# Seven edits to the gate and hidden stages of a fused block (RG-LRU attention and ternary FFN): w_out split early, VectorE order, two high parts of g from PSUM

## The reference

```python
xn = layernorm(x)
# attention branch (RG-LRU)
y = gelu(xn @ w_y + b_y)
xb = xn @ w_x + b_x
conv = conv_b + sum(conv_w[k] * shifted(xb, 3 - k) for k in range(4))
gate_x = sigmoid(conv @ w_ig + b_ig)
gate_a = sigmoid(conv @ w_ag + b_ag)
log_a = -8.0 * gate_a * softplus(a_param)
a = exp(log_a)                         # 0 for the first token
mult = sqrt(1.0 - exp(2.0 * log_a))    # 1 for the first token
h[t] = a[t] * h[t-1] + gate_x * conv * mult
attn = (h * y) @ w_out + b_out
# FFN branch, weights replaced by {-1, 0, 1} times their mean absolute value
g = silu(xn @ w1q.T) * (xn @ w3q.T)    # 682 hidden features
ffn = g @ w2q.T
out = x + attn + ffn
```

## Time and profile before

| | |
|---|---|
| median of 3 runs | 74.77 us |
| lowest, highest | 74.32, 74.97 us |
| the profiled execution's own time | 74.64 us |
| span of the profiled execution | 72.8 us |
| TensorE busy with matmuls | 68.1 us (93% of the span), 378 instructions |
| VectorE busy | 56.8 us (78%), 93 instructions |
| ScalarE busy | 52.5 us (72%), 81 instructions |
| GpSimd busy | 47.4 us (65%), 64 instructions |
| granted TensorE clock | full in all 40 slices |

### The profile page before, as it was taken

The page is one execution under the profiler, slowest core; times in us unless marked ns, Lnnn a source line. Parts: engine busy times, 40 slices in busy tenths (PEclk is TensorE's granted clock), DMA queues, the critical chain, the costliest instruction groups (busy, mean ns, idle before and its releaser), DMA issues.

```text
span 72.8 us, 1128 instructions
## 1 busy us (share of the span) xinstructions
PE 68.1 (93%) x378; PEld 58.9 (81%) x378; DVE 56.8 (78%) x93; ACT 52.5 (72%) x81; POOL 47.4 (65%) x64
## 2 busy tenths in 40 slices
PE   4999999899999999999999999989999999999750
PEld 4998898588888888888888878857899999999640
DVE  0386798999999999999999990994444799998360
ACT  3685777796978999999968959859989974333000
POOL 6277736899989994000029977699599899466400
PEclk9999999999999999999999999999999999999999
DMA  0899999920000000000000000000000000000555
GB/s 6 230 295 332 361 377 395 382 99 0 9 0 0 4 0 0 0 0 0 0 0 9 0 0 9 0 0 0 1 0 0 0 0 0 9 0 0 200 193 183
DMA packets 5112, 5.63 MB, mean 77 GB/s; under 512 B 541, under 2 KB 4594, under 8 KB 5106
## 3 DMA queue, kind: packets, MB, share of 16 engines
q1 hardware_dynamic: 4818, 5.42, 22.0%
q10 hardware_dynamic: 288, 0.14, 0.7%
HBM read 4.51 MB, written 1.05 MB: 76 GB/s over the span
## 4 chain that ended last, share of the span: by engine, by line
PE 41%; DVE 17%; POOL 13%; issue 11%; ACT 9%; DMA 3%; POOLq 2%; DVEq 0%; ACTq 0%
PE slot L753 21%; PE slot L770 10%; DVE slot L649 5%; PE slot L876 4%; DVE w_raw L616 4%; ACT w_raw L404 4%; POOL rstd L263 4%; DMA par<-params 3%; POOL w_lo L247 3%; PE slot L812 3%; PE slot L779 3%; DVE gt L676 2%; DVE xn_y L544 2%; DVE slot L638 2%; POOLq L52 2%
## 5 line engine op out<-in xcount | busy, mean ns | idle before, releaser
L295 POOL TENSOR_TENSOR g_lo<-w_raw,g_hi 128x512 fp32r<-128x512 f32 x10 | 14.7, 1488 | 2.3 <-ACT g_hi L410 2.2
L770 PE MATMUL slot<-xt_hi,w_q 128*128 128x512 f32 x40 | 15.8, 396 | 0.4 <-DVE w_raw L616 0.4
L770 PE MATMUL slot<-xt_lo,w_q 128*128 128x512 f32 x40 | 15.7, 393 | 0.0
L616 DVE SCALAR_TENSOR_TENSOR w_raw<-w_raw,s,slot 128x512 f32<-128x512 f32 x10 | 7.2, 746 | 5.2 <-ACT w_raw L404 5.2
L802 PE MATMUL slot<-w_q,g_lo 128*128 128x256 f32 x40 | 9.7, 283 | 0.0
L802 PE MATMUL slot<-w_q,g_hi 128*128 128x256 f32 x40 | 9.7, 283 | 0.0
L770 PEld LDWEIGHTS slot<-xt_hi,w_q 128*128 128x128 f32 x40 | 7.5, 188 | 2.6 <-DVE w_raw L616 1.0
L594 DVE SCALAR_TENSOR_TENSOR conv<-slot,par,conv 128x511 f32<-128x511 f32 (+2 forms) x12 | 9.0, 748 | 0.4
L770 PEld LDWEIGHTS slot<-xt_lo,w_q 128*128 128x128 f32 x40 | 7.5, 188 | 1.7
L242 POOL CAST w_hi<-w_raw 128x512 fp32r<-128x512 f32 x3 | 1.8, 614 | 9.7 <-DVE mult L628 9.7
L410 ACT ACTIVATE g_hi<-w_raw 128x512 fp32r<-128x512 f32 x9 | 5.7, 629 | 3.2 <-DVE w_raw L616 3.2
(11 more groups left out here) (125 smaller groups left out, 171.9 us busy)
## 6 DMA issues: line engine op xcount, KB each, us to landing
w_raw<-w13t SPq DMA_DIRECT2D x2, 682.0 KB, 6.5
w_raw<-dense SPq DMA_DIRECT2D x5, 256.0 KB, 4.4
out<-x_sb SPq DMA_DIRECT2D x3, 256.0 KB, 2.2
w_raw<-w2t SPq DMA_DIRECT2D x1, 640.0 KB
x_sb<-x SPq DMA_DIRECT2D x4, 128.0 KB, 2.2
x_sb<-x SPq DMA_DIRECT2D x2, 256.0 KB, 3.7
out<-x_sb ACTq DMA_DIRECT2D x1, 128.0 KB, 2.1
out<-x_sb SPq DMA_DIRECT2D x1, 128.0 KB, 1.7
```

What stands on the lines that cost most here:

```text
L295: nc.gpsimd.tensor_tensor(g_lo[:, j, s], g[:, n % RING], g_hi[:, j, s].bitcast(f32), ALU.subtract).then_inc(g_lo_set, 1)
L616: nc.vector.scalar_tensor_tensor(out=g[:, n % RING], in0=silu[:, n % RING], scalar=s32[:, 0:1], in1=slot[H_SLOT[s][j]][:, 1], op0=ALU.mult ...
L770: mm = nc.tensor.matmul(slot[H_SLOT[s][j]][:, o], w13_q[:, c, col:col + P], v[:, s, c], start=(c == 0 and v is xt_hi), stop=(c == KC - 1 a ...
```

## The change

- ScalarE casts w_hi of w_out behind conv_hi(0,0), with a semaphore of its own, and the high part of b_out behind `gelu_of(0)`. Before, GpSimd cast the first behind the squares, and ScalarE the second behind g_hi(4).
- GpSimd sets the pads of `gt` (the first 32 partitions before anything else, the other 32 behind conv_lo(0,0)), makes w_lo of w_out behind conv_lo(0,1) and the low part of b_out between conv_lo(1,0) and conv_lo(1,1). `half_biases` and `rates` come behind w_lo of w_out.
- VectorE makes the gated input of sequence 1 right behind that of sequence 0, ahead of `ternary_w2`. It makes g(5) ahead of `tail_lo`.
- VectorE makes g_hi(8) and g_hi(9) itself with a second L616-like instruction from PSUM and silu; before, ScalarE cast the one and GpSimd the other. `first_root` follows each.
- ScalarE makes the tail's silu ahead of g_hi(0), and the other high parts one product later than their silu.
- `down(1)` waits for the new semaphore of g_hi(8), `project` for that of w_lo of w_out.

```diff
+        ON_ACT = 2 * FULL - 2
...
@@ GpSimd @@
+            nc.gpsimd.memset(gt[32:HALF].bitcast(f32), 1.0).then_inc(gt_pads_set, 1)
+            pool.wait_ge(gt_pads_set, 1)
...
             lo_of_conv(0, 0)
+            pool.wait_ge(conv_lo_set, 1)
+            nc.gpsimd.memset(gt[96:P].bitcast(f32), 0.0).then_inc(gt_pads_set, 1)
+            pool.wait_ge(gt_pads_set, 2)
+            lo_of_conv(0, 1)
+            pool.wait_ge(wout_hi_set, 1)
+            nc.gpsimd.tensor_tensor(w_lo[:, WOUT], w_raw[:, WOUT], w_hi[:, WOUT].bitcast(f32), ALU.subtract).then_inc(wout_lo_set, 1)
             half_biases()
             rates()
-            lo_of_conv(0, 1)
-            gt_pads(slice(32, HALF), 1.0, KC)
-            pool.wait_ge(gt_pads_set, 1)
             lo_of_conv(1, 0)
-            gt_pads(slice(96, P), 0.0, KC + 1)
-            pool.wait_ge(gt_pads_set, 2)
+            pool.wait_ge(b_hi_set, 1)
+            nc.gpsimd.tensor_tensor(b_split[:, 1], b_row[:, :], b_split[:, 0].bitcast(f32), ALU.subtract).then_inc(b_split_set, 1)
             lo_of_conv(1, 1)
-            pool.wait_ge(a2_set, SEQS)
-            square_hi(WOUT)
-            square_lo(WOUT)
             for n in range(2 * FULL):
-                if n == 2 * FULL - 1:
-                    pool.wait_ge(g_set, n + 1)
-                    nc.gpsimd.tensor_copy(g_hi[:, HJ[n][1], HJ[n][0]], g[:, n % RING]).then_inc(g_hi_set, 1)
                 lo_of_g(n)
...
@@ ScalarE @@
             conv_hi_of(0, 0)
+            act.wait_ge(w_loaded[WOUT], 16)
+            nc.scalar.activation(w_hi[:, WOUT], w_raw[:, WOUT], ACT.Copy).then_inc(wout_hi_set, 1)
             newest_tap(1)
             conv_hi_of(0, 1)
             gelu_of(0)
+            act.wait_ge(b_out_loaded, 16)
+            nc.scalar.activation(b_split[:, 0], b_row[:, :], ACT.Copy).then_inc(b_hi_set, 1)
             conv_hi_of(1, 0)
...
-            g_hi_of(0)
             act.wait_ge(t_psum, 1)
             act.wait_ge(w2_q_set, 1)
             nc.scalar.activation(silu_t[HALF:HALF + TAIL], slot[TAIL_SLOT][0:TAIL].rearrange("p s n -> p (s n)"), ACT.Silu,
                                  scale=scale[0:TAIL, 0:1]).then_inc(silu_t_set, 1)
...
+            g_hi_of(0)
+            for n in range(2, 2 * FULL):
                 silu_of(n)
-                if n > FULL:
+                if n <= ON_ACT:
                     g_hi_of(n - 1)
-                if n == FULL + 1:
+                if n == FULL - 1:
+                    tail_hi(gt_hi[HALF:HALF + TAIL])
+                if n == FULL + 2:
                     tail_hi(gt[0:TAIL])
...
@@ VectorE @@
+            def g_hi_end(n):
+
+                s, j = HJ[n]
+                nc.vector.scalar_tensor_tensor(out=g_hi[:, j, s], in0=silu[:, n % RING], scalar=s32[:, 0:1],
+                                               in1=slot[H_SLOT[s][j]][:, 1], op0=ALU.mult, op1=ALU.mult).then_inc(g_hi_end_set, 1)
...
             gated_input(0)
+            gated_input(1)
             ternary_w2()
             squares(0)
             squares(1)
             g_of(0)
             g_of(1)
-            gated_input(1)
             tail_product()
...
+            for n in range(2, ON_ACT):
                 g_of(n)
+                if n == FULL:
+                    tail_lo()
+            for n in range(ON_ACT, 2 * FULL):
+                g_of(n)
+                g_hi_end(n)
+                dve.wait_ge(g_hi_end_set, n - ON_ACT + 1)
+                first_root(0, n - ON_ACT)
...
@@ TensorE @@
             down(0)
-            pe.wait_ge(g_set, 9)
+            pe.wait_ge(g_hi_end_set, 1)
             down(1)
-            pe.wait_ge(w_lo_set, KC * (WOUT + 1))
+            pe.wait_ge(wout_lo_set, 1)
             project(0, range(len(O_TILES[0])))
```

More of the change, by code:

```diff
@@ L162, in build @@
         w_lo_set = sem("w_lo_set")
+        wout_hi_set, wout_lo_set = sem("wout_hi_set"), sem("wout_lo_set")
+        g_hi_end_set = sem("g_hi_end_set")
         sp_abs, sp_exp, sp_log, rate_set, half_b_set = (
@@ L238, in _ @@
             nc.gpsimd.memset(abs_sum[:, 3:4], 0.0).then_inc(consts_set, 1)
+            pool.wait_ge(gaps_set, 2)
+            pool.wait_ge(ident_set, 1)
+            pool.wait_ge(power_set, 1)
+            pool.wait_ge(consts_set, 2)
+            nc.gpsimd.memset(gt[32:HALF].bitcast(f32), 1.0).then_inc(gt_pads_set, 1)
+            pool.wait_ge(gt_pads_set, 1)
             def square_hi(m):
@@ L281, in half_biases @@
                 nc.gpsimd.tensor_scalar(half_b[:, :], par[:, B_IG:B_IG + 2 * KC], 0.5, None, ALU.mult).then_inc(half_b_set, 1)
-            def gt_pads(rows, value, chunk):
-                pool.wait_ge(conv_lo_set, chunk)
-                nc.gpsimd.memset(gt[rows].bitcast(f32), value).then_inc(gt_pads_set, 1)
             def lo_of_conv(s, c):
@@ L293, in lo_of_g @@
                 s, j = HJ[n]
-                pool.wait_ge(g_hi_set, n + 1)
+                if n < ON_ACT:
+                    pool.wait_ge(g_hi_set, n + 1)
+                else:
+                    pool.wait_ge(g_hi_end_set, n - ON_ACT + 1)
                 nc.gpsimd.tensor_tensor(g_lo[:, j, s], g[:, n % RING], g_hi[:, j, s].bitcast(f32), ALU.subtract).then_inc(g_lo_set, 1)
@@ L313, in _ @@
             lo_of_conv(0, 0)
+            pool.wait_ge(conv_lo_set, 1)
[4 more added lines that the diff above has]
+            nc.gpsimd.tensor_tensor(w_lo[:, WOUT], w_raw[:, WOUT], w_hi[:, WOUT].bitcast(f32), ALU.subtract).then_inc(wout_lo_set, 1)
             half_biases()
             rates()
-            lo_of_conv(0, 1)
-            gt_pads(slice(32, HALF), 1.0, KC)
-            pool.wait_ge(gt_pads_set, 1)
             lo_of_conv(1, 0)
-            gt_pads(slice(96, P), 0.0, KC + 1)
-            pool.wait_ge(gt_pads_set, 2)
+            pool.wait_ge(b_hi_set, 1)
+            nc.gpsimd.tensor_tensor(b_split[:, 1], b_row[:, :], b_split[:, 0].bitcast(f32), ALU.subtract).then_inc(b_split_set, 1)
             lo_of_conv(1, 1)
-            pool.wait_ge(a2_set, SEQS)
-            square_hi(WOUT)
-            square_lo(WOUT)
             for n in range(2 * FULL):
-                if n == 2 * FULL - 1:
-                    pool.wait_ge(g_set, n + 1)
-                    nc.gpsimd.tensor_copy(g_hi[:, HJ[n][1], HJ[n][0]], g[:, n % RING]).then_inc(g_hi_set, 1)
                 lo_of_g(n)
-                if n == FULL - 1:
-                    pool.wait_ge(b_hi_set, 1)
-                    nc.gpsimd.tensor_tensor(b_split[:, 1], b_row[:, :], b_split[:, 0].bitcast(f32), ALU.subtract).then_inc(b_split_set, 1)
             def gated_products(c):
@@ L494, in _ @@
                                  scale=scale[0:TAIL, 0:1]).then_inc(silu_t_set, 1)
[L495 to L505, removed]
+            g_hi_of(0)
+            for n in range(2, 2 * FULL):
                 silu_of(n)
-                if n > FULL:
+                if n <= ON_ACT:
                     g_hi_of(n - 1)
-                if n == FULL + 1:
+                if n == FULL - 1:
+                    tail_hi(gt_hi[HALF:HALF + TAIL])
+                if n == FULL + 2:
                     tail_hi(gt[0:TAIL])
-            g_hi_of(2 * FULL - 2)
-            silu_of(2 * FULL - 1)
             for s in range(SEQS):
@@ L515, in _ @@
                     mult_of(s, c)
-            act.wait_ge(g_set, 2 * FULL)
+            act.wait_ge(g_hi_end_set, 2)
             nc.scalar.activation(state(1, 0), ta[:, 1, 0], ACT.Copy).then_inc(a_psum, 1)
@@ L711, in _ @@
             g_of(1)
-            gated_input(1)
             tail_product()
[L714 to L718, removed]
-                g_of(n)
[L720 to L724, removed]
+            for n in range(2, ON_ACT):
+                g_of(n)
+                if n == FULL:
[5 more added lines that the diff above has]
+                first_root(0, n - ON_ACT)
             for s in range(SEQS):
```

## The result

| | before | changed |
|---|---|---|
| median | 74.56 us (4 runs) | 75.71 us (4 runs) |
| lowest, highest | 74.32, 74.97 | 75.46, 75.99 |
| ratio, 95% interval | | 1.0156 [1.0121, 1.019] |
| the profiled execution: time, span | 74.64, 72.8 | 75.89, 74.1 |

The forecast was 76.4 with a range of 74.3 to 77.1, and slower as the likeliest. The loss has the place that was forecast, but it comes out of two errors that partly cancel.

What follows compares the result with a forecast made beforehand. TensorE and the scan chain, within 0.7 us of each other, bound the kernel. 74.64 + 3.0 (conv_lo(1,1) stall) - 0.66 (hidden pause) - 0.72 (last wait) gave 76.3, on the median 76.4; own range 75.9 to 76.9, whole range 74.3 to 77.1.

Steps and rivals of the forecast that it cites:

- the variant with b_out exempt: Gate stage: if b_out's one-partition read takes no turn, conv_lo(1,1) ends at 29.7 and the loss is 1.0 instead of 3.0.
- L566 #2 +1.44 to 30.6; conv_lo(1,1) +1.14 to 31.7: Gate stage: behind b_out's low part VectorE takes the turn, then conv_lo(1,1) ends at 31.7; TensorE loses 3.0; chance 0.45.
- rival A: Gate stage: a_rate gets in ahead of L563 #1, conv_lo(1,1) ends at 30.3, stall 1.6, end 75.0; chance 0.30 with its variant.
- rival B: Gate stage: GpSimd keeps the access from b_out's low part on, conv_lo(1,1) is in time by 28.85, end 73.8; chance 0.18.
- hidden, with 0.2 to spare: Behind the last silu: VectorE's two L616 and root memset (1.9) fit within ScalarE's 2.1 to the first product.
- (f): End of hidden stage: g_hi 8 and 9 on VectorE are hidden, and the last silu no longer waits for g_hi(8).
- -0.72: End of kernel: TensorE's last wait, for the low part of h*y, goes, saving 0.72.
- Rival C: WAG product: TensorE's clock falls to half behind the 3 us pause, 12 matmuls cost 2.8 more, end 79; chance 0.07.
- (a): ScalarE before newest_tap(1): casting w_hi of w_out there, and b_out's cast before conv_hi(1,0), costs nothing, at most 0.1.
- (c): Start of kernel: setting gt's pads (0.95) in GpSimd's idle time before the parameters land costs nothing.
- (d): VectorE: gated_input(1) ahead of ternary_w2 costs nothing with 3.0 of delay; without the stall 0.15 to 0.2 lost.
- (e): Hidden stage: with g of the sixth product ahead of tail_lo, TensorE's pause at the ninth hidden product goes, -0.66.

Runs made afterwards that it cites:

- experiment 1: Changed kernel with the low part of b_out behind conv_lo(1,1) on GpSimd instead of ahead of it: 75.15 us, ratio 1.0074 to the kernel before.
- experiment 4: Changed kernel with GpSimd's gate stage put back as in the kernel before, the rest left changed: 73.95 us, ratio 0.9921 to the kernel before.
- Experiment 2: Changed kernel with b_out's low part behind conv_lo(1,1) and, in its place, an extra GpSimd subtraction of 256 columns on 128 partitions: 78.77 us.
- experiment 10: experiment 4's kernel with the gated input of sequence 1 put back behind g(1): 73.98 us, ratio 0.9924 to the kernel before.
- experiment 9: Kernel before with one edit, g(5) ahead of tail_lo on VectorE: 74.34 us, ratio 0.9964.
- experiment 3: Changed kernel with b_out's low part behind conv_lo(1,1) and, in its place, an extra GpSimd subtraction of 256 columns on 96 partitions: 75.85 us.
- experiment 5: Changed kernel with an extra one-column square root on ScalarE behind the last silu, waiting for nothing: 75.34 us, ratio 1.0092 to the kernel before.

## Why the prediction was right, and where it was not

**Right in place and kind.** That VectorE's ternary instructions and GpSimd's take whole turns, that four of GpSimd's now stand beside four of VectorE's, and that conv_lo(1,1) is what TensorE misses near 29 us: experiments 1 and 4 show it. Up to the low part of b_out the working held within 0.15: a_rate 25.2 (25.26), L563 #2 25.9 (26.02), conv_lo(1,0) 27.05 (27.17), L566 #1 28.55 (28.65), b_out 29.15 (29.24). The open question was a read on one partition: it is held like any other (2.11 instead of 0.73), so the variant with b_out exempt is out. In this the trace agrees with the Trainium skill, "SBUF — State Buffer", section "Who interferes with whom", which makes no exception for so narrow a read. The rows of the kernel before pointed that way already: it isn't so that only operations on 128 partitions collided there, since the memset on 32 partitions took 1.58 beside L563 instead of 0.95.

**The step that was mis-sized: "L566 #2 +1.44 to 30.6; conv_lo(1,1) +1.14 to 31.7".** It passed the turn to VectorE on the strength of rows on 128 partitions. Behind b_out's part, on one partition, GpSimd went straight on: 30.45, a stall of 1.7 instead of 3.0. That is the size of rival A's stall (1.6), but A's order did not occur: L559 #1 was through at 25.17, ahead of a_rate. That GpSimd kept the access is what rival B asked of it, only it happened after the second L563 and the first L566 had both had their turns, so it didn't save the stall. Experiment 2 is the forecast's own case: conv_lo(1,1) at 31.79 against 31.7.

**The step that failed: "hidden, with 0.2 to spare", in (f), and with it the last term, -0.72.** The working compared when VectorE and ScalarE reach the first product, and there it held (VectorE is through with its second memset at 57.47, 2.0 behind the end of the last silu). But it took the table load for free behind the last silu, and the load is part of the first mult, and that waits for `first_root`, which now stands behind g_hi(8). The load moved by 0.58. The last silu was also reckoned at the end of the tenth hidden product, where ScalarE reached it 0.45 later, by way of tail_lo, g(6) and the tail's second copy. So the scan chain moved by +1.2, as much as TensorE, and the last wait stayed.

In sum: forecast +3.0 - 0.66 - 0.72 = +1.6; measured in the profiled executions +1.7 - 0.66 = +1.1 on TensorE, and +1.2 with a last wait that is 0.1 longer. One error of 1.3 too much and one of 0.8 too little. The median moved by 1.15. That the time came out so near the forecast is luck in part: it lies under 75.9 to 76.9, the forecast's own range, and within the whole range only because that reached down to rival A, whose order did not occur. Another 0.2 of the distance to 76.4 is the base, 74.77 when the forecast was made and 74.56 over the four runs. One of the named signs, that TensorE would not wait for conv_lo at the end, did not come.

**Rival C** had the right mechanism and too high a price. With the wait really at 2.8 (experiment 2) the clock fell, and it cost 1.5, not 2.8: of the 12 matmuls the first three paid next to nothing, five paid 0.20 each, and the last four 0.13 each, as the clock came back among them. In the changed kernel, with 1.44 of wait, the clock stayed full beside it. Parts (a), (c), (d) and (e) are worth what was said: no wait stands before newest_tap(1), the pads are out of the way, experiment 10 gives nothing for (d), and hidden(8) doesn't wait, though experiment 9 shows that this took more than the one edit named.

## What to carry to other kernels

Before an instruction is put into a "free" place on GpSimd, write down what VectorE runs there, and let the two go in turns on paper, by their ends; the cost falls on whoever needs the last of GpSimd's. Idle time was at hand here: GpSimd had over 9 us of it between 28 and 38 us, and the same work there cost nothing (experiment 4). And ask of every wait on ScalarE whether a table load hides behind it: one dummy activation ahead of the wait gave 0.36 us here.

## What the runs showed of the hardware

- With GpSimd's next instruction already issued, a waiting VectorE instruction got the turn behind a GpSimd subtraction on 128 partitions (experiment 2, and the earlier trace rows); behind one on 96 (experiment 3) or on one partition (the changed kernel, experiment 5) GpSimd's next instruction kept it. The three operations of 256 columns took 2.11 each and ended within 0.04 of each other. Experiments 2 and 3 are one execution each.
- ScalarE's load of the square root's table (1.28) stood behind the wait of the first square root: in the changed kernel it began 0.58 behind the silu's end. With an activation of the same function in front, which waits for nothing, it began at once (experiment 5).
- TensorE's granted clock went from full to half about 1.2 us after a wait of 2.8, with matmuls running again, and was back by 36.7 (experiment 2, one execution); after a wait of 1.44 it did not fall (the changed kernel, experiment 3).
